# First sequence's feed-forward and the second layer's first queries done tile by tile, with the inverse roots of that stretch on GpSimd

## The chip, the cores and the metric

One core of one Trainium2 chip runs the whole program. The metric is the device time of one execution in microseconds (us), here always of that one core; a profiled execution is used for the rows. The engines are TensorE (PE, with its weight loads as PEld), VectorE (DVE), ScalarE (ACT), GpSimd (POOL) and SyncE (SP), which issues nearly all transfers.

## What is computed

Two sequences of 256 rows (D = 256) pass through two layers. Layer 0 is a cross attention with 16 heads over a context of 4096 rows, a gated convolution block, and a feed-forward with quantised inputs. Layer 1 is a cross attention over the same context with one head, then a self attention and a mixture of experts. The change lies in the feed-forward of layer 0 and the cross attention of layer 1:

```python
def _L0_ffn_ref(x, ...):
    h = layernorm(x, ln1_g, ln1_b)
    h = bitlinear(h, w1, b1)                # 256 -> 1024, rows scaled and rounded to -128..127
    h = jax.nn.gelu(h, approximate=False)
    h = layernorm(h, ln2_g, ln2_b)
    h = bitlinear(h, w2, b2)                # 1024 -> 256
    return h
def _L1_xattn_ref(q, k, v, att_mask, Wq, bq, Wk, bk, Wv, bv):
    ...
    att_score = jnp.einsum('bqd,bkd->bqk', wq, wk) / SCALE + att_mask
    att_weight = jax.nn.softmax(att_score, axis=-1)
    return jnp.einsum('bqk,bkd->bqd', att_weight, wv)
x = x + _L0_attn_ref(_layernorm(x, axis=-1), ...)
x = x + _L0_ffn_ref(_layernorm(x, axis=-1), ...)
x = x + _L1_xattn_ref(_layernorm(x, axis=-1), ctx_1024, ctx_1024, mask_SxS2_ff0, ...)
```

## The kernel before

Every engine's program is written out by hand, and the engines hand work to each other through counting semaphores. Each engine executes strictly in the order of its text. The 512 rows of x are four tiles of 128 rows: tiles 0 and 1 are the first sequence, 2 and 3 the second.

In the stretch of the change TensorE finishes the gated convolution of the second sequence (`fuse(1, m)`, `project_out(1)`) with the first sequence's up-projection (`project_up(0, n)`) between. Then it runs alone through the rest of the first sequence's feed-forward: `turn_hidden` transposes a quantised hidden tile, `project_down` multiplies it by the second weight matrix, and then the first sequence's normalised rows are turned (`turn_half`), projected to queries, and the queries are folded into the key weights (`fold_queries`), so that the scores can be taken straight against the context. VectorE does all the normalising and quantising between. Scores come next: a unit w of `key_scores(w, n)` is one tile of queries against 4096 context rows, in 8 pieces of 512. VectorE adds the mask to each piece and takes its maximum (`mask_unit`); three PSUM banks are used in turn, so piece n waits for the mask of piece n - 3. Among the scores of units 0 and 1 stands the second sequence's feed-forward. ScalarE takes the exponentials of a whole unit (`key_exps`), TensorE turns them (`turn_exps`), ScalarE and VectorE copy them out (`copy_exps`), and `weigh_context` sums up the context rows. Units 2 and 3 (the second sequence) follow.

A layer norm needs the inverse root of a variance. VectorE asks for it (`ask_root`, semaphore `ln_var`), ScalarE takes a square root (`root`, semaphore `ln_sd`) and VectorE a reciprocal (`take_root`). In this stretch both tiles of a sequence are always normalised together.

SyncE's order there: the context rows of the first sequence (4 MB) when `fuse(1, 3)` is done, then two mask pieces of 1 MB when `project_out(1)` is done, and the further masks as VectorE frees their places.

## Time and profile before

| | |
|---|---|
| median of 3 runs | 991.32 us (986.51 to 995.81) |
| profiled execution | 990.4 us, its span 988.4 us |
| TensorE | 896.7 us busy, 91% of the span |
| VectorE | 608.3 us, 62% |
| ScalarE | 480.2 us, 49% |
| GpSimd | 105.9 us, 11% |
| chain that ended last | 79% TensorE, 8% VectorE, 6% ScalarE, 4% issue, 2% transfers |

The span is what the rows are timed in, from the first to the last instruction; 2.0 us of the execution lie outside it. Busy time is summed over instructions, and TensorE's records are as long as the engine had them in its pipe, so that 91% busy is not 91% of its peak. TensorE's granted clock (PEclk) is 1.00 at 2.4 GHz and 0.50 at 1.2 GHz.

### The profile page before, as it was taken

What the parts mean: (1) busy time and instruction counts of PE and PEld (TensorE: products, weight loads), DVE (VectorE), ACT (ScalarE), POOL (GpSimd) and SP (SyncE); (2) the same over time, 40 slices, a digit from 0 to 9 for tenths busy, and PEclk for the clock granted to TensorE, in tenths of its full rate; (3) what the DMA queues carried; (4) which work ended last, traced back from release to release, by engine and by line L of the source; (5) the groups of instructions that cost most, each with busy time, mean ns of one, the idle gap of its engine ahead of it and who ended that gap; (6) DMA issues with size and microseconds to landing.
All of it is one profiled execution on the core that took longest, in us unless ns stands there. A gap on an engine that the chain in (4) does not pass through costs nothing.

```text
span 988.4 us, 15292 instructions
## 1 busy us (share of the span) xinstructions
PE 896.7 (91%) x5986; PEld 528.0 (53%) x5988; DVE 608.3 (62%) x1083; ACT 480.2 (49%) x953; POOL 105.9 (11%) x118
## 2 busy tenths in 40 slices
PE   6787699999999999999998899679899999989878
PEld 3354444444455555554544586444684784555735
DVE  3876477788885446888844386846624217368442
ACT  2232266777775556777788552324322210567211
POOL 1421001111000000000000200100000005335100
PEclk9999799999999999999999999959899999999979
DMA  9672724345322101221603710523644732000000
GB/s 358 214 203 98 252 80 126 110 148 155 119 65 81 60 33 56 74 65 65 206 3 122 261 53 1 169 88 128 213 170 151 274 110 62 1 0 2 1 1 22
DMA packets 68837, 108.70 MB, mean 110 GB/s; under 512 B 7062, under 2 KB 42902, under 8 KB 66838
## 3 DMA queue, kind: packets, MB, share of 16 engines
q1 hardware_dynamic: 67372, 101.92, 31.5%
q10 hardware_dynamic: 1392, 5.77, 1.5%
q8 instruction: 50, 0.82, 0.3%
q14 instruction: 23, 0.19, 0.1%
HBM read 93.77 MB, written 13.89 MB: 109 GB/s over the span
## 4 chain that ended last, share of the span: by engine, by line
PE 79%; DVE 8%; ACT 6%; issue 4%; DMA 2%; SPq 0%; POOL 0%; ACTq 0%; DVEq 0%
PE psum L1819 13%; PE psum L1801 11%; PE psum L1772 10%; PE psum L2188 6%; PE psum L2161 5%; PE psum L1950 5%; PE psum L1754 5%; PE psum L1744 5%; PE psum L2281 4%; PE psum L1963 3%; ACT arena L749 3%; DVE arena L1112 2%; PE psum L2335 2%; PE psum L2320 1%; PE psum L2353 1%
## 5 line engine op out<-in xcount | busy, mean ns | idle before, releaser
L1112 DVE TENSOR_REDUCE arena<-psum 128x1 f32<-128x1024 f32 x256 | 300.6, 1218 | 111.3 <-PE psum L1772 111.2
L749 ACT ACTIVATE arena<-psum 128x512 f32<-128x512 f32 x512 | 264.7, 603 | 63.3 <-PE psum L1801 62.3
L1801 PE MATMUL psum<-arena 99*128 99x256 bf16 x1024 | 161.0, 275 | 10.4 <-ACT arena L749 4.8
L1772 PE MATMUL psum<-arena 96*128 96x512 bf16 x512 | 152.2, 383 | 18.0 <-DVE arena L1112 11.4
L1801 PEld LDWEIGHTS psum<-arena 99*128 99x128 bf16 x1024 | 80.0, 97 | 109.2 <-ACT arena L749 50.6
L1819 PE MATMUL psum<-arena 128*32 128x256 f32 x2048 | 136.8, 385 | 0.0
L1819 PEld LDWEIGHTS psum<-arena 128*32 128x32 f32 x2048 | 53.5, 109 | 75.4 <-ACT arena L749 36.9
L1744 PE MATMUL psum<-arena 128*128 128x512 f32 x128 | 64.1, 629 | 5.9 <-DMA arena<-ctxT 5.9
L1772 PEld LDWEIGHTS psum<-arena 96*128 96x128 bf16 x512 | 49.3, 99 | 35.6 <-DVE arena L1112 18.8
L1754 PE MATMUL psum<-arena 128*128 128x256 f32 x256 | 64.1, 395 | 1.0 <-ACT arena L727 1.0
L648 POOL TENSOR_TENSOR arena<-arena 128x512 bf16<-128x512 f32 x34 | 41.6, 1222 | 210.2 <-DVE arena L1098 202.5
L2188 PE MATMUL psum<-arena 128*128 128x256 f32 x256 | 59.9, 389 | 0.0
L1754 PEld LDWEIGHTS psum<-arena 128*128 128x128 f32 x256 | 48.6, 195 | 19.5 <-issue 13.4
L2161 PE MATMUL psum<-arena 128*128 128x512 f32 x128 | 56.0, 593 | 0.0
L726 ACT ACTIVATE arena<-psum,arena 128x512 bf16<-128x512 f32 x32 | 22.0, 688 | 66.2 <-PE psum L1744 49.6
L732 ACT ACTIVATE arena<-psum 128x512 f32<-128x512 f32 x32 | 19.1, 598 | 70.9 <-PE psum L1754 70.9
L2188 PEld LDWEIGHTS psum<-arena 128*128 128x128 f32 x256 | 49.1, 196 | 6.6
L1950 PE MATMUL psum<-arena 128*128 128x256 f32 x192 | 47.0, 404 | 3.5 <-ACT arena L813 0.9
L1950 PEld LDWEIGHTS psum<-arena 128*128 128x128 f32 x192 | 38.2, 202 | 11.1 <-ACT arena L921 1.3
L2281 PE MATMUL psum<-arena 128*128 128x512 f32 x96 | 41.9, 594 | 0.7 <-ACT arena L914 0.7
L1963 PE MATMUL psum<-arena 128*128 128x256 f32 (+1 forms) x160 | 36.6, 388 | 4.2 <-ACT arena L909 2.2
L1744 PEld LDWEIGHTS psum<-arena 128*128 128x128 f32 x128 | 24.6, 202 | 29.6 <-issue 22.2
(244 smaller groups left out, 954.3 us busy)
## 6 DMA issues: line engine op xcount, KB each, us to landing
arena<-kparts SPq DMA_DIRECT2D x192, 128.0 KB, 3.0
kparts<-arena SPq DMA_DIRECT2D x32, 384.0 KB, 3.0
arena<-ctxT SPq DMA_DIRECT2D x21, 512.0 KB, 5.2
arena<-ctx SPq DMA_DIRECT2D x2, 4096.0 KB, 15.5
arena<-mask SPq DMA_DIRECT2D x8, 1024.0 KB, 5.3
arena<-mask ACTq DMA_DIRECT2D x4, 1024.0 KB, 13.1
arena<-ctxT SPq DMA_DIRECT2D x1, 4096.0 KB, 13.6
arena<-ctxT SPq DMA_DIRECT2D x4, 1024.0 KB, 8.3
```

The costliest lines, as they stand in the source:

```text
L749: nc.scalar.activation(PR[step % 4][:, pair * CH:(pair + 1) * CH], ring_bank(slot), ACT.Exp)\
L1112: nc.vector.tensor_reduce(MX[g % 2][:, col:col + 1], unit_banks(n).rearrange("p b n -> p (b n)"), AX.X, ALU.max).then_inc(s_maxed, 1)
L1744: last = nc.tensor.matmul(ring_bank(slot), WK[:, k, f * P:(f + 1) * P], CTX[n % SLOTS][:, k, :], start=(k == 0), stop=(k == CT - 1))
L1754: last = nc.tensor.matmul(ring_bank(slot)[:, v * 256:(v + 1) * 256], CTX[n % SLOTS][:, k, (2 * i + v) * P:(2 * i + v + 1) * P], WV[:, k, : ...
L1772: last = nc.tensor.matmul(out, q, KST[g % 2][0:ROWS, j, at], start=True, stop=not masked, skip_group_check=True)
L1801: last = nc.tensor.matmul(ring_heads(slot)[:, u, :], KST[gg % 2][0:KROWS, j, kc * P:(kc + 1) * P], QST[0:KROWS, G * g + j, b * S:(b + 1) * S],
L1819: last = nc.tensor.matmul(PV[32 * j:32 * (j + 1), :], V_flat[:, at:at + 32], PR[step % 4][:, j * S:(j + 1) * S], start=(kc == 0), stop=(kc ...
L1950: last = nc.tensor.matmul(out, weights[:, k, m * P:m * P + width], xs[k], start=(k == 0), stop=(k == n - 1))
L1963: last = nc.tensor.matmul(out, lhs[k], weights[:, k, :], start=(k == 0 and not biased), stop=(k == n - 1), skip_group_check=biased)
L2161: last = nc.tensor.matmul(psum[:, unit % 3, :], QC[:, c, w * P:(w + 1) * P], CTXT[w // 2][:, c, n * 512:(n + 1) * 512], start=(c == 0), st ...
L2188: last = nc.tensor.matmul(psum[:, 6, 0:256], PT1[:, k * P:(k + 1) * P], CTXK[w // 2][:, k, :], start=(k == 0), stop=(k == KC - 1), skip_gr ...
L2281: last = nc.tensor.matmul(psum[:, bank, :], HTF[:, c, i * P:(i + 1) * P], WQKV[which][:, c, half * HALF:(half + 1) * HALF], start=(c == 0) ...
```

## The change

The first sequence's two tiles go through the feed-forward one after the other. VectorE normalises and quantises tile 0 alone, TensorE turns it in front of `fuse(1, 0)` and projects it up between `fuse(1, 0)` and `fuse(1, 1)`, and tile 1 follows between `fuse(1, 1)` and `fuse(1, 3)`. After the output projection TensorE takes tile 0 down, turns it, projects and folds its queries (`turn_tile`, `queries_tile`, `fold_tile`), and starts on the scores of unit 0. Tile 1's down-projection, queries and fold stand between the pieces of unit 0, and the second sequence's up-projection moves from unit 0's to unit 1's pieces. In this stretch every inverse root is one instruction on GpSimd, a power of -0.5 (`power`, 9 of them), in place of ScalarE's square root and VectorE's reciprocal. ScalarE's Gelu function is asked for once ahead of need. The centring of hidden tile 1, done by ScalarE and GpSimd before, is done by VectorE (`gain(1)`, `shift(1)`); tile 3's stays on ScalarE and GpSimd.

The diff, without the helpers' new signatures:

```diff
-            for b in range(B):
-                pool.wait_ge(on["d_centred"], b + 1)
-                odd = UH[2 * b + 1][:, 0, :]
-                nc.gpsimd.tensor_tensor(odd, odd, row("g2"), ALU.mult).then_inc(on["d_gained"], 1)
+            powers = [2 + 1]
+            pool.wait_ge(built, 9)
+
+            def power(first, last):
+
+                powers[0] += 1
+                pool.wait_ge(ln_var, powers[0])
+                part = SD[:, 4 + first:4 + last]
+                nc.gpsimd.tensor_tensor(part, part, NHALF[:, first:last], ALU.pow).then_inc(ln_sd, 1)
+
+            power(0, 1)
+            power(1, 2)
+            power(0, 1)
+            power(1, 2)
+            power(0, 1)
+            power(2, 4)
+            power(1, 2)
+            power(2, 4)
+            pool.wait_ge(on["d_centred"], 1)
+            odd = UH[3][:, 0, :]
+            nc.gpsimd.tensor_tensor(odd, odd, row("g2"), ALU.mult).then_inc(on["d_gained"], 1)
+            power(2, 4)
...
-            copy_quantised(0)
-            gelus(0)
-            root(0, 2)
-            centre_odd(0)
+            sqrts[0] += POWERS
+            copy_quantised_tile(0)
+            gelus(0, 2)
+            copy_quantised_tile(1)
+            gelus(2, 4)
             copy_hidden(0)
+            copy_turned_tile(0)
+            copy_queries_tile(0)
+            copy_folded_tile(0)
             copy_hidden(1)
-            root(2, 4)
-            root(0, 2)
-            copy_turned_half(0)
-            copy_queries(0)
-            copy_folded(0)
+            copy_turned_tile(1)
+            copy_queries_tile(1)
+            copy_folded_tile(1)
             copy_quantised(1)
-            gelus(1)
             key_exps(0)
-            root(2, 4)
-            centre_odd(1)
+            gelus(4, 8)
             copy_exps(0, 0)
             copy_exps(0, 2)
+            centre_odd(3)
             key_exps(1)
+            copy_exps(0, 4)
             copy_hidden(2)
-            copy_exps(0, 4)
             copy_exps(0, 6)
+            copy_exps(1, 0)
             copy_hidden(3)
-            copy_exps(1, 0)
             copy_exps(1, 2)
-            root(2, 4)
             copy_exps(1, 4)
             copy_turned_half(1)
             copy_exps(1, 6)
-            copy_queries(1)
-            copy_folded(1)
+            copy_queries()
+            copy_folded()
...
-            add_mixed(0)
-            ask_root(0, 2, 1.0 + 1e-5, 1e-5 * 1e-5)
-            take_root(0, 2)
+            add_mixed(0, 1, TT)
+            add_mixed(1, 2, TT + 1)
             dve.wait_ge(on["rows_loaded"], 48)
-            normalise_for_up(0)
-            for m in range(3):
-                gate(1, m)
-            for n in range(4):
-                hidden(0, n)
+            for i in range(2):
+                take_power()
+                normalise_for_up(i)
+            hidden(0, 0)
+            hidden(0, 1)
+            gate(1, 0)
+            gate(1, 1)
+            hidden_stats(0, 0)
+            hidden_stats(0, 1)
+            aggregate(2, 0, 1)
+            ask_root(0, 1)
+            gate(1, 2)
+            hidden(0, 2)
+            hidden(0, 3)
             gate(1, 3)
-            for n in range(4):
-                hidden_stats(0, n)
-            aggregate(2, 0, 2)
-            ask_root(0, 2)
-            add_down_bias(0)
-            take_root(0, 2)
-            turn_means(0)
             gain(0)
-            for i in range(2):
-                shift(i)
-                find_scale(i)
-                quantise_hidden(i)
-            add_mixed(1)
-            ask_root(2, 4, 1.0 + 1e-5, 1e-5 * 1e-5)
-            take_root(2, 4)
-            add_down(0)
-            ask_root(0, 2)
-            take_root(0, 2)
+            take_power()
+            shift(0)
+            find_scale(0)
+            quantise_hidden(0)
+            hidden_stats(0, 2)
+            hidden_stats(0, 3)
+            aggregate(2, 1, 2)
+            ask_root(1, 2)
+            add_down_bias(0, 1)
+            gain(1)
+            take_power()
+            done()
+            add_down(0, 1, TT + 2)
+            shift(1)
             centre_for_keys(0)
-            normalise_for_up(1)
-            copy_cq(0)
-            dve.wait_ge(on["e_cq_copied"], 1)
+            find_scale(1)
+            quantise_hidden(1)
+            add_mixed(2, 4, TT + 3)
...
-                if 2 <= n < 6:
-                    hidden(1, n - 2)
+                if n == 0:
+                    add_down(1, 2, TT + 5)
+                    take_power()
                 if n == 1:
-                    add_down_bias(1)
-                if n == 6:
-                    hidden_stats(1, 0)
-                    hidden_stats(1, 1)
+                    centre_for_keys(1)
+                    copy_cq(0, 0, 1)
+                if n == 2:
+                    normalise_for_up(2)
+                if n == 5:
+                    normalise_for_up(3)
                 if n == 7:
-                    hidden_stats(1, 2)
+                    copy_cq(1, 1, 2)
             bias_exps(0)
             for n in range(8):
                 mask_unit(1, n)
-                if n == 0:
-                    hidden_stats(1, 3)
-                    aggregate(2, 2, 4)
-                    ask_root(2, 4)
+                if 1 <= n < 5:
+                    hidden(1, n - 1)
                 if n == 4:
-                    take_root(2, 4)
-                    turn_means(1)
-                if n == 5:
-                    gain(2)
-                if n == 6:
-                    shift(2)
+                    add_down_bias(2, 3)
+                if n >= 5:
+                    hidden_stats(1, n - 5)
             bias_exps(1)
+            copy_exps(0, 1)
+            hidden_stats(1, 3)
+            aggregate(2, 2, 4)
+            ask_root(2, 4)
+            copy_exps(0, 3)
+            take_power()
+            turn_mean(3)
+            gain(2)
+            shift(2)
+            copy_exps(0, 5)
             find_scale(2)
-            copy_exps(0, 1)
             quantise_hidden(2)
-            copy_exps(0, 3)
+            copy_exps(0, 7)
             shift(3)
             find_scale(3)
-            copy_exps(0, 5)
+            copy_exps(1, 1)
             quantise_hidden(3)
-            copy_exps(0, 7)
-            copy_exps(1, 1)
             norm_att(0)
-            add_down(1)
-            ask_root(2, 4)
             copy_exps(1, 3)
-            take_root(2, 4)
-            centre_for_keys(1)
+            add_down(2, 4, None)
             copy_exps(1, 5)
+            centre_for_keys(2, 3)
             copy_exps(1, 7)
-            copy_cq(1)
+            copy_cq(2, 2, 4)
...
                 pe.wait_ge(on["c_hb_copied"], 4)
+                turn_quantised(0, 0)
                 fuse(1, 0)
-                fuse(1, 1)
-                turn_quantised(0)
-                fuse(1, 2)
                 pe.wait_ge(on["x_ready"], TT + 2)
                 pe.wait_ge(on["d_turned_copied"], 1)
                 pe.wait_ge(on["w_quantised"], 6)
-                for n in range(4):
-                    project_up(0, n)
+                project_up(0, 0)
+                project_up(0, 1)
+                fuse(1, 1)
+                turn_quantised(0, 1)
+                fuse(1, 2)
+                pe.wait_ge(on["d_turned_copied"], 2)
+                project_up(0, 2)
+                project_up(0, 3)
                 fuse(1, 3)
...
-            for i in range(2):
-                turn_hidden(i)
-                project_down(i)
-
-            pe.wait_ge(on["x_ready"], 2 * TT + 2)
+            turn_hidden(0)
+            project_down(0)
             pe.wait_ge(on["l1w_loaded"], 64)
-            turn_half(HLE, 0, 2 * TT)
+            turn_tile(HLE, 0, 2 * TT)
             turned()
-            project_queries(0)
-            fold_queries(0)
-            bias_queries(0)
-            pe.wait_ge(on["e_qc_copied"], CT)
-            turn_quantised(1)
+            queries_tile(0)
+            fold_tile(0)
+            turn_hidden(1)
+            pe.wait_ge(on["e_qc_copied"], 1)
...
-            for n in range(8):
-                key_scores(0, n)
-                if 1 <= n < 5:
-                    if n == 1:
-                        pe.wait_ge(on["d_turned_copied"], 2)
-                    if n >= 3:
-                        pe.wait_ge(on["d_hidden"], 4 + n - 2)
-                    project_up(1, n - 1)
+            key_scores(0, 0)
+            bias_tile(0)
+            project_down(1)
+            key_scores(0, 1)
+            key_scores(0, 2)
+            key_scores(0, 3)
+            turn_tile(HLE, 1, 2 * TT)
+            key_scores(0, 4)
+            turned()
+            queries_tile(1)
+            key_scores(0, 5)
+            pe.wait_ge(on["e_cq_copied"], 1)
+            fold_tile(1)
+            key_scores(0, 6)
+            bias_tile(1)
+            key_scores(0, 7)
+            turn_quantised(1, 0, 1)
+            pe.wait_ge(on["e_qc_copied"], 2)
             for n in range(8):
                 key_scores(1, n)
+                if n < 4:
+                    if n == 0:
+                        pe.wait_ge(on["d_turned_copied"], 3)
+                    if n >= 2:
+                        pe.wait_ge(on["d_hidden"], 4 + n - 1)
+                    project_up(1, n)
...
             weigh_context(0, 0)
-            pe.wait_ge(on["d_hidden"], 8)
-            turn_hidden(2)
             turn_exps(0, 4)
             turn_exps(0, 5)
             weigh_context(0, 1)
+            pe.wait_ge(on["d_hidden"], 8)
+            turn_hidden(2)
             turn_exps(0, 6)
             turn_exps(0, 7)
+            weigh_context(0, 2)
             project_down(2)
-            weigh_context(0, 2)
-            turn_hidden(3)
             turn_exps(1, 0)
             turn_exps(1, 1)
             weigh_context(0, 3)
-            project_down(3)
+            turn_hidden(3)
             turn_exps(1, 2)
             turn_exps(1, 3)
             weigh_context(1, 0)
+            project_down(3)
```

TensorE's order behind the output projection of the second sequence, before. L2036 is `turn_hidden`, L1963 `project_down`, L1941 `turn_half`, L1950 the queries and the fold, L2056 `bias_queries`, L2021 `turn_quantised`, L2161 `key_scores`, L2029 `project_up`:

```order
L2135 UNCONDITIONAL_BRANCH
L2036 MATMUL psum<-arena 128x128 x8
L1963 MATMUL psum<-arena 128x256 x8
L2036 MATMUL psum<-arena 128x128 x8
L1963 MATMUL psum<-arena 128x256 x8
L1941 MATMUL psum<-arena 128x128 x4
L1950 MATMUL psum<-arena 128x256 x8
L2056 MATMUL psum<-arena 128x1 x4
L2021 MATMUL psum<-arena 128x128 x4
L2161 MATMUL psum<-arena 128x512 x4
L2029 MATMUL psum<-arena 128x512 x2
```

The same place in the changed program, where L2091 is `turn_hidden`, L2018 `project_down`, L2104 `turn_tile`, L2005 the queries and the fold, L2239 `key_scores` and L2119 `bias_tile`:

```order
L2217 UNCONDITIONAL_BRANCH
L2091 MATMUL psum<-arena 128x128 x8
L2018 MATMUL psum<-arena 128x256 x8
L2104 MATMUL psum<-arena 128x128 x2
L2005 MATMUL psum<-arena 128x128 x8
L2091 MATMUL psum<-arena 128x128 x8
L2239 MATMUL psum<-arena 128x512 x2
L2119 MATMUL psum<-arena 128x1 x2
L2018 MATMUL psum<-arena 128x256 x8
L2239 MATMUL psum<-arena 128x512 x6
L2104 MATMUL psum<-arena 128x128 x2
```

One tile's down-projection, its turn, queries and fold now stand behind the first piece of scores and not in front of it.

VectorE's order from the last gated product to the quantising of hidden tile 0, before (L1307 `gate(1, 3)`, L1385 `hidden_stats`, L1391 `add_down_bias`, L1400 `gain`, L1410 `shift`):

```order
L1307 SCALAR_TENSOR_TENSOR arena<-psum,arena 128x256 [waits c_fuse]
L1385 BN_STATS arena<-arena 128x6 [waits d_gelu] x4
L1261 BN_AGGR arena<-arena 128x2 [waits step_v]
L1261 BN_AGGR arena<-arena 128x2
L1247 TENSOR_SCALAR arena<-arena 128x2 [waits step_v]
L1391 TENSOR_TENSOR arena<-arena 128x256 [waits step_v]
L1391 TENSOR_TENSOR arena<-arena 128x256
L1240 RECIPROCAL arena<-arena 128x2 [waits ln_sd]
L1395 SCALAR_TENSOR_TENSOR arena<-arena 128x2 [waits step_v]
L1400 SCALAR_TENSOR_TENSOR arena<-arena 128x1024
L1410 SCALAR_TENSOR_TENSOR arena<-arena 128x1024 [waits step_v]
```

And in the changed program, from the gated products on (L1361 `gate`, L1430 `hidden_stats`, L1295 `ask_root`, L1423 `hidden`, L1443 `gain`, L1453 `shift`):

```order
L1361 SCALAR_TENSOR_TENSOR arena<-psum,arena 128x256 [waits c_fuse] x2
L1430 BN_STATS arena<-arena 128x6 [waits d_gelu] x2
L1309 BN_AGGR arena<-arena 128x2 [waits step_v]
L1295 TENSOR_SCALAR arena<-arena 128x1 [waits step_v]
L1361 SCALAR_TENSOR_TENSOR arena<-psum,arena 128x256 [waits c_fuse]
L1423 SCALAR_TENSOR_TENSOR arena<-psum,arena 128x512 [waits d_up] x2
L1361 SCALAR_TENSOR_TENSOR arena<-psum,arena 128x256 [waits c_fuse]
L1443 SCALAR_TENSOR_TENSOR arena<-arena 128x1024
L1453 SCALAR_TENSOR_TENSOR arena<-arena 128x1024 [waits ln_sd,step_v]
```

Hidden tile 0's statistics have moved in front of the last gated product; its gain and shift follow directly.

GpSimd's order in this stretch in the changed program (L690 is `power`, L702 the gain of hidden tile 3; before, the only row there is the second of these, twice):

```order
L690 TENSOR_TENSOR arena<-arena 128x1 [waits ln_var,built]
L690 TENSOR_TENSOR arena<-arena 128x1 [waits ln_var] x4
L690 TENSOR_TENSOR arena<-arena 128x2 [waits ln_var]
L690 TENSOR_TENSOR arena<-arena 128x1 [waits ln_var]
L690 TENSOR_TENSOR arena<-arena 128x2 [waits ln_var]
L702 TENSOR_TENSOR arena<-arena 128x1024 [waits d_centred]
L690 TENSOR_TENSOR arena<-arena 128x2 [waits ln_var]
```

Nine powers are new on GpSimd, and one of its two gains has gone.

## Rows read from the trace of the kernel before

**Rows 1.** Windows of the stretch: busy us of each engine (instructions), PEclk, transfers' share, GB/s

```profile
634.00:664.00 30.00, 15.62 (x65) 11.07 (x66) 19.65 (x50) 5.46 (x10) 3.36 (x1) 0.60 0.49 174
...
706.00:743.00 37.00, 36.53 (x214) 32.36 (x212) 9.18 (x21) 10.13 (x16) 0.00 (x0) 1.00 0.39 151
```

**Rows 2.** Timeline of TensorE to the first scores: start, length, operation, [idle before <- releaser]

```profile
620.01 3.69 PE L1950 MATMUL psum<-arena 128*128 128x256 f32 x16 [0.66 <-ACT arena L852]
...
630.15 3.72 PE L1963 MATMUL psum<-arena 128*128 128x256 f32 x16
640.12 0.48 PE L2036 MATMUL psum<-arena 128*128 128x128 bf16 x3 [6.26 <-DVE arena L1424]
642.60 0.71 PE L2036 MATMUL psum<-arena 128*128 128x128 bf16 x5 [2.00 <-issue]
644.43 1.89 PE L1963 MATMUL psum<-arena 128*128 128x256 bf16 x8 [1.12 <-ACT arena L909]
...
654.76 3.78 PE L1950 MATMUL psum<-arena 128*128 128x256 f32 x8 [0.75 <-ACT arena L914]
...
663.94 3.65 PE L2161 MATMUL psum<-arena 128*128 128x512 f32 x8
```

**Rows 3.** Timeline of TensorE around the end of units 0 and 1, and before unit 2

```profile
674.30 19.05 PE L2161 MATMUL psum<-arena 128*128 128x512 f32 x44
...
698.96 1.09 PE L2175 MATMUL psum<-arena 128*128 128x128 f32 x4 [3.77 <-DVE arena L1502]
699.84 5.73 PE L2188 MATMUL psum<-arena 128*128 128x256 f32 x16
...
742.01 1.05 PE L2056 MATMUL psum<-arena 128*128 128x1 f32 x8 [0.47 <-ACT arena L927]
```

**Rows 4.** Windows of 1 us in which the granted clock moved (columns as above)

```profile
639.00:640.00 1.00, 0.00 (x0) 0.00 (x0) 0.97 (x3) 0.00 (x0) 0.00 (x0) 0.62 1.09 345
...
697.00:698.00 1.00, 0.00 (x0) 0.00 (x0) 0.93 (x4) 0.99 (x2) 0.00 (x0) 0.63 0.87 291
...
704.00:705.00 1.00, 1.00 (x6) 0.81 (x6) 0.15 (x2) 0.00 (x0) 0.00 (x0) 0.95 1.08 357
```

**Rows 5.** Timeline of VectorE, single rows of it

```profile
615.94 0.42 DVE L1312 TENSOR_TENSOR arena<-arena,psum 128x256 f32<-128x256 f32 x1 [1.30 <-PE psum L1963]
...
617.99 0.88 DVE L1353 SCALAR_TENSOR_TENSOR arena<-arena 128x256 f32<-128x256 f32 x2
...
622.25 0.36 DVE L1372 TENSOR_SCALAR arena<-arena 128x256 bf16<-128x256 bf16 x2
...
629.60 2.46 DVE L1385 BATCH_NORM_STATS2 arena<-arena 128x6 f32<-128x512 f32 x4
...
639.55 0.43 DVE L1424 TENSOR_SCALAR arena<-arena 128x1024 bf16<-128x1024 bf16 x1
...
692.50 2.65 DVE L1410 SCALAR_TENSOR_TENSOR arena<-arena 128x1024 f32<-128x1024 f32 x1
```

**Rows 6.** VectorE's groups from 610 to 745 us: count, busy us, mean ns, idle before

```profile
L1482 DVE CUSTOM_DVE_ANT_0 arena<-psum,arena 128x512 f32<-128x512 f32 x16 | 11.0, 690 | 10.1 <-PE psum L2161 10.0
...
L1341 DVE TENSOR_REDUCE arena<-arena 128x1 f32<-128x1024 f32 x4 | 4.9, 1218 | 0.1
...
L1400 DVE SCALAR_TENSOR_TENSOR arena<-arena 128x1024 f32<-128x1024 f32 x2 | 2.6, 1280 | 0.0
```

**Rows 7.** GpSimd's groups by form

```profile
L678 POOL TENSOR_TENSOR arena<-arena 128x1024 f32<-128x1024 f32 x2 | 6.8, 3375 | 126.2 <-ACT arena L904 126.2
L671 POOL TENSOR_SCALAR arena<-arena 128x16 f32<-128x16 f32 x16 | 4.8, 326 | 0.1
```

**Rows 8.** The line of ScalarE's square roots from 610 to 730 us: times, first and last start

```profile
L802 ACT ACT_TABLE_LOAD  x4: 1283/1283/1283, 611.7 to 722.3; - x4
```

**Rows 9.** Transfers issued from 625 to 650 us, with the median us to landing

```profile
arena<-ctx SPq DMA_DIRECT2D x1, 4096.0 KB, 15.3
arena<-mask SPq DMA_DIRECT2D x2, 1024.0 KB, 12.1
```

More of the change, by code:

```diff
@@ L1262, in aggregate, with take_power, add_to_x @@
                 done()
-            def add_to_x(name, n, add, first=0, last=TT):
+            def take_power():
+                roots[0] += 1
+                dve.wait_ge(ln_sd, roots[0])
+            def add_to_x(name, n, add, first=0, last=TT, ahead=None):
+                ahead = TT * n + first if ahead is None else ahead
                 for i in range(first, last + 1):
@@ L1356, in normalise_for_up @@
                 done()
-                for i in two:
-                    mark(nc.vector.scalar_tensor_tensor(out=HLQ[:, i % 2, :], in0=HLQ[:, i % 2, :],
-                                                        scalar=SD[:, 4 + i:5 + i], in1=row("b1"),
-                                                        op0=ALU.mult, op1=ALU.add))
+                mark(nc.vector.scalar_tensor_tensor(out=part, in0=part, scalar=SD[:, 4 + i:5 + i], in1=row("b1"),
+                                                    op0=ALU.mult, op1=ALU.add))
```

184 lines of the change are left out of this document (111 added, 73 removed).

## Prediction

> **What bounds the kernel now.** The page's chain of waits is 79% TensorE, so a change pays only where TensorE waits or runs slowly. I then read the windows of this stretch. From 706 to 743 us TensorE is busy 36.5 of 37 us at full clock; from 634 to 664 us only 15.6 of 30, at a mean granted clock of 0.60 [rows 1]. The timeline says why. The output projection ends at 633.87 (630.15 + 3.72), and the first piece of scores starts at 663.94 [rows 2], 30.1 us later. Between lies one serial chain: VectorE quantises hidden tile 0 (TensorE idle 6.26 us), then come an idle of 2.00 us with no releaser ("issue"), a copy on ScalarE (1.12), the second tile's likewise, VectorE's sums and norm, and the copies of the queries. All of it runs for TensorE at 1.2 GHz, since the clock fell in the idle, at 639 to 640 us [rows 4]. A second hole is at 695.2 to 699.0: TensorE waits 3.77 us for a copy that VectorE makes late [rows 3]; the clock falls again (697 to 698) and is back at 704 to 705 [rows 4], so the first `weigh_context` takes 5.73 us.
>
> **Part 1: to the end of the output projection, 0.** VectorE adds tile 1's output at 615.94 [rows 5]; add, statistics, aggregate and ask take 1.25 us (0.42 + 0.42 + 0.17 + 0.17 and gaps), so 617.2. The 13 instructions that quantise both tiles ran from 617.99 to 622.61 [rows 5], 4.6 us; one tile alone I put at 2.8, since the small ones do not halve. Tile 0 is then ready at 620.0, when TensorE is ready for `fuse(1, 0)`: it started at 620.01 [rows 2]. Tile 1 is ready at 622.8, in the shade of `fuse(1, 0)`, two up-projections and `fuse(1, 1)`. The same matrix work is cut differently, so the block still ends at about 633.9.
>
> **Part 2: from there to the first scores, 14.3 us earlier.** Before, VectorE went from the end of the last gated product at 629.7 through four statistics (629.60, 2.46 us), aggregates, bias, means, gain, shift, scale and rounding to 639.98 [rows 5]. The change leaves gain 1.28 [rows 6], shift 1.28, scale 1.75 (the reduction is 1.22 of it [rows 6], three small ones the rest) and rounding 1.95, 6.3 in all: ready at 636.0. TensorE turns the tile (0.45), and I keep the 2.00 us of "issue" of before, which stand right after a branch under full transfer load [rows 1, 2]: 638.6. ScalarE copies (1.12 with its wait [rows 2]), the down-projection takes 0.87 at full clock: 640.6. VectorE has meanwhile done tile 1's statistics, bias and gain (to 639.8). It adds tile 0's result, statistics and ask 1.3, the shift 1.28 that covers the root, and the centring 0.41: 643.65. Then, at the low clock: turn 0.6, copy 0.5, queries 1.7 (half of what L1950 shows for two tiles, 3.78, less overlap [rows 2]), copy 0.4, fold 1.7, `turn_hidden(1)` 0.9 (ready by VectorE at 647.4): first scores at 649.6 in place of 663.94. The copies of masks and context (1 MB and 4 MB pieces, landing 12.1 and 15.3 us after issue at 633.9 and 629.2 [rows 9]) are in at 648.5 at the latest in the trace, so they just hide; VectorE would need the first mask at 653.
>
> **Part 3: what was moved among the scores, 4.5 us.** TensorE's work from the first scores to the end of unit 1 is 16 pieces of 1.72 us (11 pieces are 19.05 less overlap [rows 3]), 27.5; four up-projections 1.7; and newly the down-projection 0.87, turn 0.22, queries and fold, bias 2 x 0.5, turn 0.24. Queries and fold of one tile are 8 records of 128 columns each where there were 8 of 256 columns for two tiles. Streaming would be 0.12 us a record, a quarter of L1950's 3.78/8 (twice the columns, half the clock [rows 2]); the row of 1-column products takes 1.05 for 8 [rows 3], 0.131 each, with hardly a column to stream. I take the latter: 2.1 us for queries and fold of tile 1. The clock: in the second hole it came back 5 us after TensorE was steadily busy again [rows 3, 4], so from 649.6 I leave it low until 653, which costs 1.7. Sum: 35.4, and unit 1 ends at 685.0 (before 693.2). VectorE must keep up: masks 16 x 0.77 [rows 6], two quantisings of 2.8, hidden 3.0, statistics 2.0, sums 2.6 are some 26 of these 35 us. The two long blocks of 2.8 between masks fit, since TensorE may be two pieces (3.4 us) ahead.
>
> **Part 4: the second hole, 5.6 back, 2.1 new.** VectorE now has nothing but one mask, one statistic and the bias of exponents ahead of its first copy: ready at 687.1, copy done at 687.8. TensorE, through its fourth turn at 688.3, has been idle 1.5 us in place of 4.1, and I take it that the clock stays; `weigh_context(0, 0)` then takes 3.46 and ends at 691.75, where it ended at 705.57. That is 13.8 us. But hidden tile 2's quantising is later against the scores than before: statistic, aggregate, copies, mean, gain 1.28, shift 2.65 (as at 692.50 beside GpSimd's 3.39; the other one beside GpSimd took 1.28 [rows 5, 7]), copy, scale, rounding end at 698.2, and TensorE arrives at `turn_hidden(2)` at 696.1. New idle 2.1 us; 0.7 if the shift takes 1.28. From there all work is as before, and TensorE has no other hole up to 743 [rows 1, 3]. `project_down(3)` and the sums come some 7 us before their use. The 4 MB of context for units 2 and 3 are asked for when x is ready, at some 715, with 16 us to land (15.3 [rows 9]): enough, barely.
>
> **Part 5: the roots.** No row shows a power on GpSimd. 16 columns of products take 0.33 us there, 1024 take 3.38 [rows 7], so one or two columns of a plain product would be under 0.33. I take 0.5 us with the hand-over, bounds 0.2 (no gain below that: nothing waits then) and 1.3, four times the row of 16 columns. The cover ahead of its use is 1.7 us at the first (tile 1's sums), 2.8, 4.1, 2.0 (bias and gain), 1.3 (the shift), 1.2, 0.7, 0.7: at 0.5 nothing is exposed, at 1.3 about 1 us. Four reloads of ScalarE's function table of 1.28 us each [rows 8] go, none on the chain; the Gelu one is now issued in ScalarE's idle at 620 us.
>
> **Sum.** 13.8 - 2.1 = 11.7 us off the profiled execution's 990.4: 978.7. The median shown is 0.9 above that execution, so 979.6, which I round to **979.5**. A measurement of this kernel tells about 1% (10 us) from no change.
>
> **Rivals.** (a) The clock works against it. TensorE's work in 636 to 650 us is thin, and the new idle times of 1.5 and 2.1 us may each bring the fall that 3.8 us brought before (it came 2.2 us into that idle [rows 3, 4]). Against: both are shorter. Price: low until 657 at the first scores +2, one later fall with some 5 us at half rate +2.5: 984. Chance 0.2.
> (b) VectorE is the bound among the scores: its work is thick there, each mask hands over, and a late quantising or hidden piece stalls the ring of three banks. For: 26 of 35 us plus waits. Against: units 0 and 1 before carried nearly as much without an idle [rows 3]. Price: each of the two long blocks exposes 1.5 us, the later ones 2: 984.5. Chance 0.12.
> (c) GpSimd's first power has a start-up cost. The 16 products of 16 columns, of one kind and with a mean of 0.33 [rows 7], show none. As a mechanism here: a first power of 6 us against a cover of 1.7 would hold TensorE 4.3 us ahead of `fuse(1, 0)`, with nothing else queued for it: 983.9. Chance 0.05. The Trainium skill, GPSIMD Engine Reference, section 2.1 Instruction dispatch, says that the first call of a freshly loaded kernel pays about 6 us without a row of its own; no run here shows it.
> (d) Slower: powers are dear every time. They run on the chain at five places with covers of 1.7, 2.0, 1.3, 0.7 and, behind slack, 1.8, so a power of L us costs 5L - 7.5. It eats the gain at L = 3.8, and from 5.8 the kernel is slower by over 1%. At 6 us: 978.7 + 22.5 = 1001. For: a power is no single-pass product and no row bounds it. Against: even 1024 columns of products take 3.4 [rows 7]. Chance 0.06.
> (e) Better: the clock never falls for long and the shift takes 1.28: 1.7 + 1.4 + 1 less, 975.5. Chance 0.1.
>
> **Chances and range.** The forecast (977 to 982) holds the remaining 0.47. The limit of 1% is 981.4, near its upper end, so of it 0.43 is faster; with (e) 0.53, and 0.04 from the low ends of (a) to (c): 0.57 faster, 0.36 within 1%, 0.07 slower. The range 973 to 988 takes in (a), (b), (c), (e) and the bounds of power, shift and clock, and leaves (d) out.
>
> **What would show it.** The first scores at about 649.6, TensorE's idle ahead of `turn_hidden(0)` 2.2 in place of 6.26, unit 1's last piece at 685, and unit 2's first at 731.4 in place of 743.1. GpSimd's powers as rows of under 1 us. Wrong, if VectorE waits on GpSimd by name, if TensorE waits for masks in units 0 and 1, if the granted clock is 0.50 beyond 655 or again after 690, or if the gain of the middle is lost after unit 2.

## The result, and the profile after

The changed kernel takes 987.69 us (median of 20 runs, 980.64 to 989.71) where the kernel before takes 993.90 (20 runs, 986.51 to 997.85): a ratio of 0.9938, interval 0.9919 to 0.9956. It is some 6 us faster, about half of what was forecast (979.5, 11.8 below the 991.32 known then); 987.69 lies near the upper end of the range, 973 to 988. The span of the profiled execution is 983.7 us, before 988.4.

Both profiles are read from T0, the end of TensorE's output projection, since what lies ahead of it is shifted by something else (last section): T0 is 633.87 before [rows 2] and 639.35 after (a row at 635.63 that lasts 3.72). TensorE after, from there to the first scores, in the columns of [rows 2]:

```profile
642.29 0.48 PE L2091 MATMUL psum<-arena 128*128 128x128 bf16 x3 [2.94 <-DVE arena L1467]
648.40 0.72 PE L2091 MATMUL psum<-arena 128*128 128x128 bf16 x5 [5.63 <-issue]
650.23 1.89 PE L2018 MATMUL psum<-arena 128*128 128x256 bf16 x8 [1.12 <-ACT arena L939]
655.88 0.66 PE L2104 MATMUL psum<-arena 128*128 128x128 f32 x2 [3.75 <-DVE arena L1330]
657.07 2.07 PE L2005 MATMUL psum<-arena 128*128 128x128 f32 x8 [0.53 <-ACT arena L950]
...
662.19 1.95 PE L2239 MATMUL psum<-arena 128*128 128x512 f32 x4
```

The wait for VectorE fell from 6.26 us to 2.94, as meant. But behind it, in the middle of `turn_hidden(0)`, stands an idle for which the profile names no releaser ("issue"); it is called the gap from here on. It grew from 2.00 us [rows 2] to 5.63. The first scores come 22.8 us after T0. Before it was 30.1, and 15.8 was forecast. The granted clock was low for nearly all of it (three windows, columns as in [rows 4]):

```profile
641.00:642.00 1.00, 0.00 (x0) 0.00 (x0) 1.00 (x3) 0.00 (x0) 0.00 (x0) 0.77 1.09 381
...
661.00:662.00 1.00, 1.00 (x9) 0.94 (x8) 0.15 (x1) 0.29 (x1) 0.70 (x1) 0.50 0.00 0
662.00:663.00 1.00, 1.00 (x7) 0.64 (x6) 0.00 (x0) 0.71 (x2) 0.00 (x0) 0.99 0.00 0
```

The second hole and what follows, in TensorE's timeline (beside [rows 3]):

```profile
698.12 0.63 PE L2251 MATMUL psum<-arena 128*128 128x128 f32 x4 [0.69 <-DVE arena L1554]
698.58 3.62 PE L2267 MATMUL psum<-arena 128*128 128x256 f32 x16
...
707.62 0.61 PE L2091 MATMUL psum<-arena 128*128 128x128 bf16 x8 [1.09 <-DVE arena L1467]
...
739.90 1.05 PE L2135 MATMUL psum<-arena 128*128 128x1 f32 x8 [0.47 <-ACT arena L975]
```

The wait of 3.77 us is down to 0.69, `weigh_context(0, 0)` runs at full clock (3.62 for 5.73), and the new wait at `turn_hidden(2)` is 1.09. Unit 2 starts at 740.95 (the end of the last row), which is 101.6 us after T0; before it was 109.2 (743.07). That is 7.6 us gained, which the times' 4.4 to 8.1 (0.9938 and its interval on 993.9) bear out.

VectorE after, in the same stretch, and one power on GpSimd:

```profile
640.98 0.43 DVE L1467 TENSOR_SCALAR arena<-arena 128x1024 bf16<-128x1024 bf16 x1
...
652.26 0.48 DVE L1470 SCALAR_TENSOR_TENSOR arena<-psum,arena 128x256 f32<-128x256 f32 x1 [7.36 <-PE psum L2018]
...
655.32 0.41 DVE L1330 TENSOR_SCALAR arena<-arena 128x256 f32<-128x256 f32 x1 [0.51 <-POOL arena L690]
```

```profile
620.93 0.57 POOL L690 TENSOR_TENSOR arena<-arena 128x1 f32<-128x1 f32 x1 [59.06 <-DVE arena L1297]
...
653.69 1.52 POOL L690 TENSOR_TENSOR arena<-arena 128x1 f32<-128x1 f32 x1 [9.91 <-DVE arena L1295]
```

VectorE had the tile ready at 641.41, 2.1 us after T0, yet TensorE's first three products start at 642.29 only; and later VectorE stood idle for 7.36 us, waiting for TensorE. The nine powers take 0.55 to 0.75 us, but for one of 1.52 (the second row), which makes VectorE wait 0.51 us.

### The profile page after: what moved, and what is told of

The parts are those of the page before. It is cut to its first block, busy times and chain, and to the rows that moved or that the text cites. A ratio compares the mean times of both kernels' runs of the same rounds, so it can differ in the third digit from the quotient of the medians.

```text
span 983.7 us, 15340 instructions
## 1 busy us (share of the span) xinstructions
PE 893.8 (91%) x6004; PEld 526.7 (54%) x6004; DVE 609.9 (62%) x1089; ACT 472.2 (48%) x946; POOL 109.1 (11%) x127
## 4 chain that ended last, share of the span: by engine, by line
PE 79%; DVE 8%; ACT 6%; issue 4%; DMA 2%; POOL 0%; SPq 0%; ACTq 0%; DVEq 0%
PE psum L1874 13%; PE psum L1856 11%; PE psum L1827 10%; PE psum L2239 6%; PE psum L2267 5%; PE psum L2005 5%; PE psum L1809 5%; PE psum L1799 5%; PE psum L2376 4%; PE psum L2018 3%; ACT arena L774 3%; DVE arena L1160 2%; PE psum L2430 2%; PE psum L2415 1%; PE psum L2448 1%
## 5 line engine op out<-in xcount | busy, mean ns | idle before, releaser
L1827 PE MATMUL psum<-arena 96*128 96x512 bf16 x512 | 153.1, 385 | 18.1 <-DVE arena L1160 11.4
L1809 PE MATMUL psum<-arena 128*128 128x256 f32 x256 | 63.5, 392 | 1.0 <-ACT arena L752 1.0
L2267 PE MATMUL psum<-arena 128*128 128x256 f32 x256 | 57.8, 379 | 0.0
L2239 PE MATMUL psum<-arena 128*128 128x512 f32 x128 | 57.2, 595 | 0.0
L2005 PE MATMUL psum<-arena 128*128 128x256 f32 (+1 forms) x208 | 47.5, 387 | 2.5 <-ACT arena L838 0.9
L2005 PEld LDWEIGHTS psum<-arena 128*128 128x128 f32 x208 | 40.0, 206 | 9.8 <-ACT arena L838 1.2
L1799 PEld LDWEIGHTS psum<-arena 128*128 128x128 f32 x128 | 24.6, 201 | 29.6 <-issue 22.5
L2018 PE MATMUL psum<-arena 128*128 128x256 f32 (+1 forms) x160 | 36.8, 389 | 3.1 <-ACT arena L836 1.4
## 6 DMA issues: line engine op xcount, KB each, us to landing
arena<-ctxT SPq DMA_DIRECT2D x1, 4096.0 KB, 13.3
```

The source lines that it names most:

```text
L1799: last = nc.tensor.matmul(ring_bank(slot), WK[:, k, f * P:(f + 1) * P], CTX[n % SLOTS][:, k, :], start=(k == 0), stop=(k == CT - 1))
L1809: last = nc.tensor.matmul(ring_bank(slot)[:, v * 256:(v + 1) * 256], CTX[n % SLOTS][:, k, (2 * i + v) * P:(2 * i + v + 1) * P], WV[:, k, : ...
L1827: last = nc.tensor.matmul(out, q, KST[g % 2][0:ROWS, j, at], start=True, stop=not masked, skip_group_check=True)
L2005: last = nc.tensor.matmul(out, weights[:, k, m * P:m * P + width], xs[k], start=(k == 0), stop=(k == n - 1))
L2018: last = nc.tensor.matmul(out, lhs[k], weights[:, k, :], start=(k == 0 and not biased), stop=(k == n - 1), skip_group_check=biased)
L2239: last = nc.tensor.matmul(psum[:, unit % 3, :], QC[:, c, w * P:(w + 1) * P], CTXT[w // 2][:, c, n * 512:(n + 1) * 512], start=(c == 0), st ...
```

## The experiments

In the table, "scores" and "unit 2" are the us from T0 to the first scores and to unit 2 in each profiled execution, "gap" is the idle without a releaser in front of the rest of the first `turn_hidden` (in e4 and e10 it stands among the fillers ahead of that turn). Each ratio is to the kernel before as timed beside that run, 17 to 23 times; the runs themselves were timed 4 to 12 times (e5 4, e8 5), and e1 to e4, e5 to e8, and e9 with e10 were timed together.

| run | ratio to before | gap | scores | unit 2 |
|---|---|---|---|---|
| before | 1 | 2.00 | 30.1 | 109.2 |
| after | 0.9938 [0.9919, 0.9956] | 5.63 | 22.8 | 101.6 |
| e1 after, context and masks late | 0.9873 [0.9837, 0.9908] | 0.47 | 15.8 | 94.6 |
| e2 before, context and masks late | 1.0000 [0.9974, 1.0026] | 0 | 26.7 | 106.0 |
| e3 after, scalar roots | 0.9923 [0.9893, 0.9953] | 5.92 | 22.5 | 101.3 |
| e4 as e1, with fillers | 0.9833 [0.9792, 0.9874] | 2.28 | 15.2 | 94.0 |
| e5 after, context alone late | 0.9861 [0.9809, 0.9913] | 0.71 | 16.2 | 95.0 |
| e6 as e1, scalar roots | 0.9891 [0.9859, 0.9923] | 0 | 16.9 | 96.1 |
| e7 as e1, tile 1 in front | 0.9971 [0.9950, 0.9992] | 0.51 | 27.2 | 103.7 |
| e8 after, masks alone late | 0.9917 [0.9877, 0.9956] | 5.73 | 22.9 | 101.7 |
| e9 before, context alone late | 1.0007 [0.9981, 1.0032] | 0 | 29.5 | 109.2 |
| e10 as e5, with fillers | 0.9884 [0.9857, 0.9911] | 1.88 | 14.8 | 93.6 |

**e1 and e2: the transfers asked for late.** The gap stands behind the branch at the end of the block (`UNCONDITIONAL_BRANCH` in TensorE's order), while the context (4 MB) and the first masks (2 MB) are in flight. In both kernels SyncE's requests were moved behind the first turn of hidden tile 0 (in e1 the context is asked for at 638.50, 4.4 us after T0, in the changed kernel 4.7 us ahead of it):

```diff
-            sp.wait_ge(on["c_fuse"], 2 * IT)
-            load(CTXK[0], ...)
             sp.wait_ge(on["c_out"], 4)
+            sp.wait_ge(on["d_turned2"], 1)
...
-            for n in range(5):
+            for n in range(2):
+                load_mask(n)
+            load(CTXK[0], ...)
+            for n in range(2, 5):
                 load_mask(n)
```

> The changed kernel, with the first two mask pieces and the 4 MB of context asked for only once TensorE has turned hidden tile 0 (before: the context after fuse(1, 3), the masks after the output projection). Theory A: the 5.63 us without a releaser inside the first turn of a hidden tile are TensorE's instructions, fetched through the same transfer engines as the 4 MB and 2 MB of data; then the gap shrinks to under 0.5 us, the first scores come 4 to 5 us earlier after the output projection (18 us in place of 22.8), and the kernel gains 3 to 5 us on the changed one (ratio to before 0.989 to 0.991). Theory B: the gap belongs to the branch itself and not to the data in flight; then it stays at 5 to 6 us, the scores come as late as now, and the first mask, now later, may cost up to 2 us more (ratio 0.994 to 0.997).

> The kernel before, with the same later requests. Theory A: its 2.00 us of the same kind go too, and the second tile's quantising, which VectorE ends at 644.85, then bounds the turn; so 0.5 to 2 us are gained (ratio 0.998 to 0.9995). Theory B: no change in the gap, ratio 1.000. Under either theory the masks are there in time, since the first mask is wanted 24 us after this place.

TensorE's timeline in e1:

```profile
636.31 0.33 PE L2093 MATMUL psum<-arena 128*128 128x128 bf16 x3 [2.21 <-DVE arena L1469]
637.10 0.45 PE L2093 MATMUL psum<-arena 128*128 128x128 bf16 x5 [0.47 <-issue]
638.67 1.17 PE L2020 MATMUL psum<-arena 128*128 128x256 bf16 x8 [1.12 <-ACT arena L941]
643.60 0.66 PE L2106 MATMUL psum<-arena 128*128 128x128 f32 x2 [3.76 <-DVE arena L1332]
...
649.88 1.97 PE L2241 MATMUL psum<-arena 128*128 128x512 f32 x4
```

With the requests late the changed kernel does what was forecast of it: first scores 15.8 us after T0, and a ratio of 0.9873, 12.6 us of 993 (interval 9 to 16). The context is used from unit 0's `weigh_context` on and nothing waits for it. In the kernel before the same edit moves nothing that the times can tell.

**e5 and e8: which transfer.** e5 moves the context alone behind that turn and leaves the masks; e8 the masks alone:

```diff
 # e5
-            sp.wait_ge(on["c_fuse"], 2 * IT)
-            load(CTXK[0], ...)
             sp.wait_ge(on["c_out"], 4)
...
             load_mask(0); load_mask(1)
+            sp.wait_ge(on["d_turned2"], 1)
+            load(CTXK[0], ...)
 # e8
             load(CTXK[0], ...)
             sp.wait_ge(on["c_out"], 4)
+            sp.wait_ge(on["d_turned2"], 1)
```

> The changed kernel with only the 4 MB of context asked for later (once hidden tile 0 is turned); the two mask pieces (2 MB) are asked for at the end of the output projection as in the changed kernel. The gap without a releaser ahead of the second transposition of hidden tile 0 was 5.63 us with 4 + 2 MB in flight and 0.47 us with none. Theory 'instructions behind the branch wait for the bulk transfers': with 2 MB in flight from T0 (end of the output projection) they land about 6 us after T0, so a gap of 1 to 3 us stands there, the first scores come 17 to 19 us after T0, and the ratio is 0.985 to 0.992. Rival 'only the large context transfer does it': gap of 0.5 us, first scores 15.8 us after T0, ratio 0.987. Rival 'it is the number of requests, not the bytes': gap as in the changed kernel, 5 us.

> The mirror image: context (4 MB) asked for as in the changed kernel, some 5 us before T0, and only the masks asked for late (once hidden tile 0 is turned). Theory 'the instructions wait until the bulk transfers have landed': 4 MB alone take 10 to 12 us, to 5 to 7 us after T0, so the gap is 2 to 4 us in place of 5.63 and the first scores come 18 to 20 us after T0. Rival 'it is the requests standing right at the branch (the masks)': the gap is gone, first scores 15.8 us after T0, ratio 0.987. Rival 'the context alone does all': gap of 5 to 6 us, ratio 0.993.

The row behind the gap, first in e5, then in e8:

```profile
634.49 0.45 PE L2093 MATMUL psum<-arena 128*128 128x128 bf16 x5 [0.71 <-issue]
```

```profile
648.47 0.72 PE L2092 MATMUL psum<-arena 128*128 128x128 bf16 x5 [5.73 <-issue]
```

The context is what does it: without it in flight at T0 the gap goes, without the masks it stays to a tenth. (The masks of e5 do not acquit masks in general: their packets start in the window 632.0 to 632.5, the one of the second packet described next.) My first theory (the instructions wait until all the bulk has landed, so that each megabyte counts) was wrong in both runs: 0.71 us where it had 1 to 3, 5.73 where it had 2 to 4. The packets of the instruction queue show more. These are the transfers' queues (packets, MB, share of 16 engines) in a window of half a microsecond, 645.5 to 646, of the changed kernel, and then in 634.5 to 635 of e1:

```profile
q1 hardware_dynamic: 166, 0.17, 107.1%
q8 instruction: 1, 0.02, 14.2%
```

```profile
q8 instruction: 1, 0.02, 13.3%
```

In every run with a gap TensorE goes on 2.4 to 3 us behind such a packet of 0.02 MB: after 648.40 behind 645.5, before 642.60 behind one at 640.0, e1 637.10 behind 634.5, e5 634.49 behind 632.0, e8 648.47 behind 645.5 (each the start of a half-microsecond window). It is the second of two, and the context holds back both. Without the context in flight the first comes 2.2 to 3.1 us ahead of T0 and the second 0.1 to 0.8 behind it (e1, e2, e4 to e7, e9, e10); with it the first comes within half a microsecond of T0 and the second at T0 + 6.1 to 6.4 (before, after, e3, e8). The first packets of after and of e1, in 639.5 to 640 and in 631.5 to 632:

```profile
q8 instruction: 1, 0.02, 11.4%
...
q8 instruction: 1, 0.02, 10.9%
```

The second packet itself takes about the same time in the two windows further up (14.2% and 13.3% of 16 engines' half microsecond, 1.1 us), so it waits ahead of its transfer. It does not wait until the bulk has landed: when it comes, the bulk runs for some 8 us more in after (to 654), but for some 3 in e8 (to 649). The Trainium skill, Runtime: NRT & Kernel Launch, section Instruction fetch mechanics, says that instructions come in blocks of 16 KiB over a transfer queue of the sequencer's own, and that a taken branch out of the two blocks at hand makes it fetch the target before it can go on. The packets of 0.02 MB around the branch agree. That they are fetched because of the branch, and not merely as the next blocks in order, no run here shows, since none moves the branch; and the view does not say for which engine a packet is. The first of them seems also to be what holds the first three products of after to 642.29, 0.9 us past VectorE's end: in e1, where it comes at 631.5 in place of 639.5, they start 0.15 us past it (636.31, 636.16).

So with the context in flight TensorE goes on at T0 + 8.7 (before, 642.60), T0 + 9.05 (after), T0 + 9.1 (e3) or T0 + 9.2 (e8); without it at T0 + 3.0 (e1, e4, e7), 3.2 (e5) or 2.5 (e10), and e6, whose turn starts at T0 + 2.40, has no gap at all.

**e9: the control in the kernel before**, the edit of e5 there.

> The kernel before with only the 4 MB of context asked for late (once hidden tile 0 is turned), the masks as they were: the control for the run of the changed kernel with the same edit. Theory 'the instructions of the block's end come 8.7 to 9.1 us behind the output projection while the context is in flight, and in the kernel before the first 6.3 us of this were covered by VectorE, which had tile 0 ready only then': here the late context gives back only the 2.0 us that stood open, less than the changed kernel's 5 us and more: the gap ahead of the second transposition is under 0.3 us, from T0 (end of the output projection) to unit 2 it is 106 us in place of 109.2, and the ratio is 0.997 to 1.000. Rival 'the late context pays everywhere alike': ratio 0.992 to 0.994.

TensorE's row at the first turn:

```profile
645.19 1.01 PE L2038 MATMUL psum<-arena 128*128 128x128 bf16 x8 [6.25 <-DVE arena L1426]
```

The turn is whole and there is no gap: VectorE's 6.25 us cover the fetch. The ratio of 1.0007 [0.9981, 1.0032] fits the first theory (0.997 to 1.000) and not the rival. The 106 us did not come: the profile has 109.2. The work up to the queries is the same as in e2, but the clock, which in e2 was back in window 662 to 663 (T0 + 23), is here at 0.88 only in:

```profile
671.00:672.00 1.00, 1.00 (x3) 0.45 (x2) 0.05 (x1) 0.00 (x0) 0.00 (x0) 0.88 0.00 0
```

That is T0 + 32, with TensorE busy without a break from 662.92: the fold takes 3.78 us for e2's 1.99, and the first eight products of the scores 5.04 for 3.65. One execution of each kernel cannot tell 3 us here.

**e4 and e10: the clock.** 32 products of 128x512 into an unused bank keep TensorE busy where it waits (10, 5, 13, 2 and 2, ahead of `turn_hidden(0)`, `project_down(0)`, `turn_tile`, `turned` and `fold_tile(0)`); e4 has them in e1, e10 in e5.

```diff
+            def keep_busy(n):
+                for _ in range(n):
+                    nc.tensor.matmul(psum[:, 2, :], IDENTB, TW1[:, 0, 0:512], start=True, stop=True)
```

> The changed kernel with the late requests of the first experiment and 32 more matrix products of 128x512 in bf16 into a free bank, 10 ahead of the first turn of a hidden tile, 5 ahead of its down-projection, 13 ahead of the turn for the queries, 2 and 2 between the query steps: they compute nothing that is used, and only fill TensorE's idle time. Theory C: the low clock of this stretch costs 3 to 4 us (the down-projection 1.89 in place of 0.87, turn and queries and fold 4.8 in place of 2.6), and with TensorE filled the granted clock stays at 2.4 GHz; then 2 to 4 us better than the first experiment (ratio 0.985 to 0.988). If the clock falls all the same, or the fillers stand in the way of work that is ready, 0 to 2 us worse than it.

> The changed kernel with the 4 MB of context late, the masks as they were, and 32 filler products of 128x512 into an unused bank where TensorE waits, so that its clock does not fall between the output projection and the scores. The fillers' results are used by nothing. It puts the two best edits together. Theory 'the clock there costs only what lies on the chain at half rate': first scores 15.0 to 15.3 us after T0 against 16.2 without fillers, ratio 0.985, no different from the run without fillers within the interval. Rival 'the clock that falls here costs more further on': ratio 0.981 or less.

In e4 the wait for VectorE at the turn and the fold after it:

```profile
644.64 0.41 PE L2106 MATMUL psum<-arena 128*128 128x128 f32 x2 [0.95 <-DVE arena L1332]
...
647.20 1.16 PE L2007 MATMUL psum<-arena 128*128 128x128 f32 x8
```

The granted clock stays at 1.00 from 632 to 660 us and the fold takes 1.16 in place of 2.08, but T0 to unit 2 shrinks only by 0.6 (e4 against e1) and 1.4 us (e10 against e5). Much of the chain there is VectorE's, and fillers may also stand in the way; the two were not told apart. By the ratios e4 is 4 us better than e1 and e10 2 us worse than e5, and the intervals of all four overlap: what the fillers bring stays open. e10's 14.8 us lie a little under the first theory's 15.0 to 15.3; its ratio, 0.9884, is above both theories'.

**e3 and e6: the roots back on ScalarE and VectorE**, all nine, once in the changed kernel and once with e1's late requests:

```diff
-            def power(first, last): ...
+            # ScalarE: root(0, 1), root(1, 2), ... at nine places; VectorE: take_root for take_power
```

> The changed kernel with all nine inverse roots of the stretch back on ScalarE and VectorE (square root, then reciprocal), tile by tile as the changed kernel asks for them, in ScalarE's order where they fall due. It tells what the powers on GpSimd are worth. If the powers are what makes the tile-wise order pay, this costs 3 to 6 us: ScalarE reloads its function tables several more times (1.28 us each), two of them ahead of the query copies on the chain (ratio 0.997 to 1.000). If the powers (0.55 to 0.75 us each, one 1.52) are no better than a square root and a reciprocal (0.2 + 0.17 us and the hand-overs), the ratio stays at 0.993 to 0.995.

> The changed kernel with context and masks asked for late, and all nine inverse roots back on ScalarE (square root) and VectorE (reciprocal), the reloads of ScalarE's table with them. The earlier run with scalar roots had the gap in front of hidden tile 0, which may have hidden what the roots cost. Theory 'the powers are worth nothing here': ratio within 0.002 of the late kernel's 0.9873, 15.8 us from T0 to the first scores. Rival 'the gap hid it': a root with its reload (1.28 us each way) lies open at tile 0's gain and at the sums behind the down-projection, first scores 17.5 to 20 us after T0 and a ratio of 0.990 to 0.992.

The copy behind the first turn in e6:

```profile
641.76 0.61 PE L2083 MATMUL psum<-arena 128*128 128x128 bf16 x8 [2.40 <-DVE arena L1459]
644.45 1.89 PE L2010 MATMUL psum<-arena 128*128 128x256 bf16 x8 [2.08 <-ACT arena L924]
```

e3 is the changed kernel over again (101.3 and 101.6 us): the powers are worth nothing that shows there. With the gap gone, tile 1's root stands in ScalarE's queue ahead of the copy of tile 0 and costs 0.96 us (2.08 against 1.12), and T0 to unit 2 is 1.5 us longer than in e1. The first scores, at 16.9, lie between the two theories' figures (15.8, and 17.5 to 20). On the other side the power's hand-over lies 0.5 us open at the centring in e1 and after. The times (0.9891 and 0.9873) cannot tell the two apart.

**e7: the part that was moved among the scores**, put in front again:

```diff
+            bias_tile(0); project_down(1); turn_tile(HLE, 1, 2 * TT); turned()
+            queries_tile(1); fold_tile(1); bias_tile(1)
+            for n in range(8):
+                key_scores(0, n)
```

> The changed kernel with the late requests, but hidden tile 1's down-projection, turn, queries, fold and bias in front of the first scores again and in one row, with VectorE's sums and centring of that tile ahead of its first mask; nothing of it stands among the scores. It keeps the tile by tile order and the powers. Theory 'the part moved among the scores is worth what its waits cost in front': down-projection .9, VectorE's sums and root 1.9, centring .4, turn .6 and its copy .5, queries and copy 1.7, fold and copy 1.7, at a low clock: first scores some 8 us later (24 us after T0), unit 0's eight pieces shorter by the 3 us of moved work, so 4 to 6 us more in all: ratio 0.991 to 0.994. Rival 'VectorE is what bounds unit 0 and 1, so it comes to the same': ratio 0.987 to 0.989.

The part in front, and the first scores:

```profile
654.17 0.66 PE L2104 MATMUL psum<-arena 128*128 128x128 f32 x2 [2.68 <-DVE arena L1332]
655.37 2.07 PE L2005 MATMUL psum<-arena 128*128 128x128 f32 x8 [0.53 <-ACT arena L952]
657.99 2.04 PE L2005 MATMUL psum<-arena 128*128 128x128 f32 x8 [0.55 <-ACT arena L959]
...
660.54 2.05 PE L2239 MATMUL psum<-arena 128*128 128x512 f32 x2
```

This is more than either theory had: 11.4 us later than e1 at the first scores and 9.1 at unit 2, in the times 9.7 (0.9971 - 0.9873). The waits of 2.68, 0.53, 0.55 and 0.55 us and the low clock come in front, and unit 0 gets only 2.3 us shorter. With the requests late in all three, T0 to unit 2 takes 106.0 us in the kernel before (e2), 103.7 in e7 and 94.6 in e1. So 9.1 of the 11.4 us stand on this overlap, and 2.3 on the rest of the change. It was tried with late requests only.

## Why the prediction was wrong, and what of it held

**The step that failed is Part 2's "I keep the 2.00 us of 'issue' of before".** I took the gap for a fixed piece to be added behind VectorE's wait. It is what is left uncovered of TensorE's wait for its next instructions, which the context in flight stretches to T0 + 8.7 and of which VectorE's 6.26 us had covered the greater part. Where I formed a sum, a maximum stood: the tile came 3.3 us sooner and the gap grew by 3.6. e5 and e8 show the cause (the context in flight; the masks are not needed for it), e9 the cover. With it cured T0 to unit 2 is 14.6 us shorter (e1) where 11.7 were forecast, and 12.6 by the times. "The copies of masks and context ... just hide" asked only whether they land in time, and not what else goes through the same queues.

To the first scores 14.3 us were forecast and 7.2 came (30.07 less 22.84), 7.1 short: the turn starts 0.8 later than in my sum (2.94 us after T0 for 2.1), the gap is 3.6 longer, turn and down-projection run at half rate where I had full clock, 1.8 (1.20 for 0.45, 1.89 for 0.87), the rest takes 10.1 for 9.0, and rounding in my sum hid 0.2. e1 takes 15.8 us, my figure, but that is luck, two errors that cancel: it reaches the end of the down-projection 1.0 us sooner than I had (its gap is 0.47 for my 2.00, its down-projection 1.17 for 0.87), and the rest again takes 10.0 for 9.0, with VectorE's wait 3.76 for my 3.0 (0.5 of it the power) and queries and fold 4.15 for 3.4.

**Part 1** held: T0 takes nearly the same values with either kernel (e1's is 634.10 and before's 633.87; after's is 639.35 and e2's 639.15), and one tile is quantised in 2.9 us (622.43 to 625.37), forecast 2.8.

**Part 3** was too dear: from the first scores to the end of unit 1 33.2 us (662.19 to 695.4), forecast 35.4. The low clock that I charged with 1.7 us was already over at 662.

**Part 4** held: the clock stayed, the 5.6 us came back, and the new wait at `turn_hidden(2)` is 1.09, within the 0.7 to 2.1 I had, since the shift beside GpSimd's gain took 1.28. From the end of unit 1 to unit 2 it takes 45.6, forecast 46.4. Together -7.1 + 2.2 + 0.8 leaves 11.7 - 4.1 = 7.6.

**Part 5** held on price (0.55 to 0.75 for my 0.5, one at 1.52 over my 1.3), and little lies open (VectorE waits 0.51 us on one power and 0.22 on another); that the powers are worth anything was not shown (e3, e6).

**The rivals.** (a), the clock, is part of what happened: low from 641 to 662 us here, worth some 1.8 of the 7.1; in e4's profile curing it brings 0.6 us. (b) did not come about: no wait of TensorE on a mask in units 0 and 1. (c) did not: the first power took 0.57 us. The Trainium skill's rule on a first call (GPSIMD Engine Reference, section 2.1) shows nowhere in these rows. (d) did not, and neither did (e), though its shift did take 1.28. Of my signs of being wrong two came: VectorE waits on GpSimd by name, and the clock was low beyond 655, to 662, though 5.5 us of that is the later T0. What came was not in my list: a bulk transfer that holds back the instructions themselves.

## What to carry to other kernels

An idle of TensorE put down to "issue" is no constant: look up when the instruction packets arrive, and treat the wait in front of it as its cover. Before making a chain shorter, ask what runs in the shade of its waits. Here a 4 MB transfer asked for 4.7 us ahead of T0 took back half the gain, and asking for it later, by 8 to 14 us in these runs, cost nothing that the times show (e2, e9). And cutting work into tiles paid mostly by what could then be put among the scores (9.1 of 11.4 us with late requests).

## What the runs showed that was not expected

The same instructions ahead of T0 take up to 8 us more or less from one execution to the next: T0 is 631.25 in e5, 633.3 to 634.1 in before, e1, e4 and e7, and 638.1 to 639.4 in the others. The windows of 560 to 565 us, before and then after, show a part of it:

```profile
560.00:565.00 5.00, 4.97 (x41) 3.76 (x44) 3.12 (x9) 1.28 (x1) 1.16 (x4) 1.00 0.99 421
```

```profile
560.00:565.00 5.00, 4.31 (x12) 3.29 (x11) 0.70 (x2) 2.07 (x3) 1.88 (x7) 0.50 1.00 421
```

In the one the clock is full, in the other it is at 0.50, and the same 16 products of an output projection take 3.72 us and 6.44:

```profile
560.03 3.72 PE L1963 MATMUL psum<-arena 128*128 128x256 f32 x16 [0.74 <-ACT arena L811]
...
560.90 6.44 PE L2018 MATMUL psum<-arena 128*128 128x256 f32 x16 [0.69 <-ACT arena L836]
```

What follows unit 2 varies too: 245.1 to 245.5 us in the three profiles of the kernel before and its variants, 242.7 to 245.4 in the nine of the changed one. Whether the change has a part in this stays open. The shift of T0 is part of why the runs of one kernel spread over 9 to 11 us (980.6 to 989.7, 986.5 to 997.9), and why intervals are read from T0 here. What decides which clock an execution gets there stays open.

Open too is what holds the instruction packets back beside the context's stream of 1 KB packets: the second comes 5 to 6 us later with it than without. SyncE is slowed in the same place: from the start of its first mask request to the end of the second it takes 5.1 us beside the context (before, after, e3) and 0.8 to 1.7 without it (e1, e5, e8, e9). Here are the rows of after and e1:

```profile
639.38 5.14 SPq L566 DMA_DIRECT2D arena<-mask  x2
...
637.64 0.82 SPq L566 DMA_DIRECT2D arena<-mask  x2
```

Whether the masks' larger packets would hold instructions back as well was not tried.
